# Scan stage of a four-part sequence model: which engine multiplies states 0 and 3 by C, and when the last normalization is applied

## What is computed

```python
# selective scan: D = 256 channels, N = 16 states
dt = softplus(x_ssm @ w_dt.T + b_dt)
Bm = x_ssm @ w_B.T + b_B;  Cm = x_ssm @ w_C.T + b_C
def step(h, inp):
    xt, dtt, bt, ct = inp
    h = exp(A * dtt[..., None]) * h + (dtt[..., None] * bt[:, None, :]) * xt[..., None]
    return h, sum(h * ct[:, None, :], axis=-1)          # y
pre = (y + D * x_ssm) * silu(z) @ w_out.T + b_out + x
x = layernorm(pre) * gamma + beta
# feed-forward, then the last normalization
h = layernorm(x) * ln_gamma + ln_beta
x = layernorm(x + 0.5 * (silu(h @ w1 + fc1_bias) @ w2 + fc2_bias))
```

## Time and profile before

| | |
|---|---|
| median of 3 runs | 1084.57 us (1084.56 to 1086.63) |
| the profiled execution's own time | 1086.53 us |
| its span, first to last instruction | 1084.6 us |
| busy in the span: PE, DVE, ACT, POOL | 977.9, 929.1, 839.2, 705.3 us |
| granted TensorE clock, mean | 0.968 of full speed |
| scan stage: first scan, last gate | 521.1 us, 1026.1 us |
| from one block's gates to the next's, blocks 3 to 6 | 63.4 us |

### The profile page before, as it was taken

One profiled execution on the slowest core, in us unless ns is written; L12 is line 12 of the kernel. 1 busy time (PEld: TensorE's weight loads), 2 busy tenths in 40 slices (PEclk: granted clock), 3 DMA queues, 4 the chain that ended last, 5 costly groups with the idle time before them and its releaser, 6 DMA issues. The chain is left out here.

```text
span 1084.6 us, 17899 instructions
## 1 busy us (share of the span) xinstructions
PE 977.9 (90%) x5612; PEld 741.5 (68%) x5612; DVE 929.1 (86%) x1234; ACT 839.2 (77%) x1633; POOL 705.3 (65%) x603
## 2 busy tenths in 40 slices
PE   5999999999987999998567699999999999997887
PEld 4677777777764555555456487777878777886676
DVE  7999999999973797866799998999999999999751
ACT  7777778888745668766876889899898988987733
POOL 3457466766761121123879998989999898999530
PEclk9999999999998999999887899999999999999999
DMA  6344434323425001111997867487776777767301
GB/s 190 122 139 120 127 120 142 115 92 118 123 59 196 0 1 59 59 40 67 243 157 193 162 156 188 134 195 157 162 162 159 178 160 183 173 140 161 82 1 39
DMA packets 87889, 137.53 MB, mean 127 GB/s; under 512 B 8818, under 2 KB 40562, under 8 KB 87796
## 3 DMA queue, kind: packets, MB, share of 16 engines
q1 hardware_dynamic: 86788, 132.73, 48.3%
q0 software_dynamic: 1008, 3.67, 1.7%
HBM read 120.12 MB, written 14.16 MB: 124 GB/s over the span
## 5 line engine op out<-in xcount | busy, mean ns | idle before, releaser
L2347 DVE TENSOR_TENSOR_SCAN oa<-bank_a,h,oa 128x512 f32<-128x512 f32 x128 | 159.8, 1270 | 13.2 <-ACT h L2033 9.8
L2347 DVE TENSOR_TENSOR_SCAN ob<-bank_a,h,ob 128x512 f32<-128x512 f32 x128 | 160.3, 1269 | 8.8 <-POOL ob L2567 5.3
L1829 PE MATMUL bank_m<-w,f_h 128*128 128x256 f32 x448 | 103.8, 381 | 0.0
L1491 POOL TENSOR_TENSOR oa<-ob,x1T 128x1024 f32<-128x1024 f32 x8 | 18.8, 2355 | 130.4 <-DVE ob L1391 130.4
L2024 ACT ACTIVATE bank_a<-s,A 128x512 f32<-128x512 f32 x128 | 86.8, 684 | 16.4 <-DVE oa L2347 10.2
L2024 ACT ACTIVATE bank_a<-dtc,A 128x512 f32<-128x512 f32 x128 | 86.8, 683 | 13.7 <-DVE oa L2347 8.1
L1769 PE MATMUL bank_y<-ident,ob 128*128 128x128 f32 x512 | 71.4, 285 | 25.3 <-POOL ob L2574 13.3
L1829 PEld LDWEIGHTS bank_m<-w,f_h 128*128 128x128 f32 x448 | 84.4, 192 | 14.1 <-issue 3.6
L1769 PEld LDWEIGHTS bank_y<-ident,ob 128*128 128x128 f32 x512 | 62.3, 147 | 36.6 <-DVE ob L2353 14.9
L1769 PE MATMUL bank_y<-ident,oa 128*128 128x128 f32 x512 | 72.1, 287 | 13.4 <-DVE oa L2353 13.4
L883 POOL TENSOR_TENSOR xd<-xs,L 128x512 f32<-128x512 f32 x32 | 33.9, 1061 | 76.6 <-DVE xs L662 76.1
(11 more groups left out here) (405 smaller groups left out, 2906.2 us busy)
## 6 DMA issues: line engine op xcount, KB each, us to landing
Bb<-CB_rows SPq DMA_DIRECT2D x128, 256.0 KB, 6.3
Cb<-CB_rows SPq DMA_DIRECT2D x128, 256.0 KB, 5.8
abc<-decays SPq DMA_DIRECT2D x32, 512.0 KB, 4.3
Ebc<-ramps SPq DMA_DIRECT2D x64, 128.0 KB, 3.1
uT<-in_uT SPq DMA_DIRECT2D x8, 512.0 KB, 4.2
u<-in_u SPq DMA_DIRECT2D x8, 512.0 KB, 3.9
x_tokens<-x2s SPq DMA_DIRECT2D x8, 512.0 KB, 3.0
x_rows<-x1T SPq DMA_DIRECT2D x8, 512.0 KB, 2.9
```

The source lines that it names most:

```text
L1829: i = e.matmul(to, f_h[:, k, c * CH:(c + 1) * CH], w2[:, k, :], start=False, stop=(c % 2 == 1 and k == KF - 1))
L2347: e.tensor_tensor_scan(s[:, k, :], p_a[k][:, :], s[:, k, :], h0[:, n, k:k + 1], ALU.mult, ALU.add).then_inc(v_s, 1)
```

## The change

Three edits. First, `on_pool` goes from `(0, 12, 14)` to `(3, 12, 14)`: VectorE makes product 0, GpSimd product 3. Counts of waits follow from the tuple. Second, the orders are changed to suit: on VectorE product 0 stands where product 1 stood and products 1 and 2 follow the scans of state 3, with both `stats3` ahead of them; on ScalarE the copies of C for states 0, 1 and 2 come at other places and the one for state 3 is gone; on GpSimd `into(5)` and `product(3)` come behind the scales. Third, `x3b` becomes two buffers, and `norm6` and `store_out` of blocks 0 to 4 are done in the following iteration, as four single instructions among the decays of states 12 to 14; block 5 stays where it was.

```diff
-            xl, (xn, x3b) = many("xl", [P, NC, DM]), (t(n, [P, NC, DM])[:, :, :] for n in ("xn", "x3b"))
+            xl, x3b, xn = many("xl", [P, NC, DM]), many("x3b", [P, NC, DM]), t("xn", [P, NC, DM])[:, :, :]
-            p_g, on_pool = d_sem("p_g"), (0, 12, 14)
+            p_g, on_pool = d_sem("p_g"), (3, 12, 14)
 # SyncE
                 def store_out(b):
                     e.wait_ge(a_n6, 4 * b + 4)
+                    after(e, st_o, DMAS * b)
...
                         load_B(cur, 11)
-                    if 0 <= old < NB - 2:
+                    if 0 <= it - 4 < NB - 3:
+                        store_out(it - 4)
+                    if old == Y - 1:
                         store_out(old)
 # ScalarE, first half of the iteration (older = it - 4)
+                    if 0 <= older < NB - 3:
+                        norm6(older, 0, (0,))
                     if live(post):
                         spread_C(post, 11)
                         decay(post, 12, 0)
...
                         decay(post, 12, 1)
+                    if 0 <= older < NB - 3:
+                        norm6(older, 0, (1,))
                     if 0 <= last < NB - 1:
                         evac_up(last, 0)
...
                         decay(post, 13, 0)
+                    if 0 <= older < NB - 3:
+                        norm6(older, 1, (0,))
+                    if live(post):
                         decay(post, 13, 1)
...
                         decay(post, 14, 0)
                         carry(post, 12)
+                    if 0 <= older < NB - 3:
+                        norm6(older, 1, (1,))
+                    if live(post):
                         decay(post, 14, 1)
 # ScalarE, second half
+                    if live(cur):
+                        spread_C(cur, 0)
                     if 0 <= post < NB - 1:
                         evac_gated(post, 0)
...
                         carry(cur, 1)
-                        spread_C(cur, 1)
                         decay(cur, 3, 0)
                         decay(cur, 3, 1)
                     if 0 <= last < NB - 2:
                         silu_up(last, 0)
                     if live(cur):
-                        spread_C(cur, 2)
+                        spread_C(cur, 1)
                     if 0 <= last < NB - 2:
                         silu_up(last, 1)
                     if live(cur):
                         silu_z(cur)
+                        spread_C(cur, 2)
...
                         decay(cur, 4, 1)
-                        spread_C(cur, 3)
                         carry(cur, 3)
...
                         decay(cur, 7, 0)
-                    if 0 <= old < NB - 2:
+                    if old == Y - 1:
                         norm6(old, 0)
+                        norm6(old, 1)
 # VectorE: x3b[b % 2] in second and stats6; second waits for the store of block b - 2
                     if live(cur):
-                        product(cur, 1)
+                        product(cur, 0)
...
                         residual(post, 1)
                         stats3(post, 0)
+                        stats3(post, 1)
                     if live(cur):
                         scan(cur, 3, 0)
+                        product(cur, 1)
                         scan(cur, 3, 1)
-                    if 0 <= post < NB - 1:
-                        stats3(post, 1)
-                    if live(cur):
                         product(cur, 2)
                     if live(cur):
                         scan(cur, 4, 0)
                         scan(cur, 4, 1)
-                        product(cur, 3)
                         scan(cur, 5, 0)
 # GpSimd: norm6 and norm36 of block b also wait until norm6 of block b - 1 is applied
                         into(cur, 2)
                         into(cur, 3)
-                        product(cur, 0)
                         into(cur, 4)
-                    if live(cur):
-                        into(cur, 5)
                     if 0 <= post < NB - 1:
                         shifted(post)
...
                         norm3(post)
                     if live(cur):
+                        into(cur, 5)
+                        product(cur, 3)
                         into(cur, 6)
                         into(cur, 7)
```

More of the change, by code:

```diff
@@ L1637, in store_out @@
                     e.wait_ge(a_n6, 4 * b + 4)
-                    e.dma_start(out.rearrange("(n p) f -> p n f", p=P)[:, b * NC:(b + 1) * NC, :], x3b).then_inc(st_o, DMAS)
+                    after(e, st_o, DMAS * b)
+                    e.dma_start(out.rearrange("(n p) f -> p n f", p=P)[:, b * NC:(b + 1) * NC, :], x3b[b % 2][:, :, :]).then_inc(st_o, DMAS)
                 def end_store(p):
@@ L2102, in silu_up, with norm6 @@
                     e.activation(part, part, ACT.Silu).then_inc(a_fs, 1)
-                def norm6(b, p):
+                def norm6(b, p, parts=(0, 1)):
                     if b in alone:
@@ L2108, in norm6 @@
                         e.wait_ge(p_l3, 4 * (b + 2) + 4)
-                    for c in (2 * p, 2 * p + 1):
-                        e.activation(x3b[:, c, :], x3b[:, c, :], ACT.Identity, bias=nb6[:, c:c + 1], scale=rs6[:, c:c + 1]).then_inc(a_n6, 1)
+                    for c in (2 * p + q for q in parts):
+                        e.activation(x3b[b % 2][:, c, :], x3b[b % 2][:, c, :], ACT.Identity, bias=nb6[:, c:c + 1], scale=rs6[:, c:c + 1]).then_inc(a_n6, 1)
                 def end_gated(p):
@@ L2150, in scalar @@
                 for it in range(NB + 3):
-                    old, last, post, cur, nxt = it - 3, it - 2, it - 1, it, it + 1
+                    older, old, last, post, cur, nxt = it - 4, it - 3, it - 2, it - 1, it, it + 1
                     if 0 < cur < NB:
@@ L2305, in scalar @@
                         carry(cur, 6)
-                    if 0 <= old < NB - 2:
-                        norm6(old, 1)
-                    if live(cur):
                         decay(cur, 7, 1)
@@ L2378, in second @@
                     e.wait_ge(pe_dn, 2 * b + p + 1)
-                    after(e, st_o, DMAS * b)
+                    after(e, st_o, DMAS * (b - 1))
                     for c in (2 * p, 2 * p + 1):
-                        i = e.scalar_tensor_tensor(x3b[:, c, :], xl[b % 2][:, c, :], twice4[b % 2][:, c:c + 1],
+                        i = e.scalar_tensor_tensor(x3b[b % 2][:, c, :], xl[b % 2][:, c, :], twice4[b % 2][:, c:c + 1],
                                                    pair[p][:, (c % 2) * DM:(c % 2 + 1) * DM], ALU.mult, ALU.add)
@@ L2390, in stats6 @@
                         e.wait_ge(p_l3, 4 * (b + 1) + 4)
-                    e.bn_stats(both_of(st6, p), turnwise(x3b, p)).then_inc(v_l6, 1)
+                    e.bn_stats(both_of(st6, p), turnwise(x3b[b % 2], p)).then_inc(v_l6, 1)
                 def end_low(p):
@@ L2596, in norm6 @@
                     e.wait_ge(v_l6, 2 * b + 2)
+                    after(e, a_n6, 4 * b)
                     scales(slice(NC, 2 * NC), p_l6, 4 * alone[b])
@@ L2600, in norm36 @@
                     e.wait_ge(v_l6, 2 * b6 + 2)
+                    after(e, a_n6, 4 * b6)
                     e.wait_ge(v_l3, 2 * b3 + 2)
```

## The result

The changed kernel took 1091.82 us (median of 6 runs, 1090.7 to 1093.65) against 1086.16 us (6 runs, 1084.56 to 1089.11) for the kernel before: a ratio of 1.0052, 95% interval 1.0036 to 1.0067. That is 5.7 us slower. In a second series of 10 runs it was 1.0038 (1.0023 to 1.0053), 4 us slower. The profiled execution took 1091.98 us, its span 1090.0.

The account below looks back on a forecast made before the run. GpSimd and VectorE were taken to pace the scan blocks within half a microsecond of each other. Blocks 0, 1, 2, 3 to 6 and 7 gave 0.4 + 2.4 + 0 + 1.8 + 0.8 = +5.4 us: 1090.0 us, range 1083 to 1093.

Parts of the forecast that it names:

- The sum: Whole kernel: block terms 0.4 + 2.4 + 0 + 1.8 + 0.8 make +5.4 us, 1090.0 us; chance 0.62 for +2.4 to +8.3.
- blocks 3 to 6: Steady blocks: GpSimd-VectorE loop grows +0.45 us each (bounds +0.1 and +0.75), together +1.8 us (0.4 to 3.0).
- both ranges: Kernel time 1083 to 1093 us overall, and 1087.0 to 1092.9 us for the forecast's own case.
- The loop: Steady block: scan (1, 0), VectorE's product 0, into(4), GpSimd's queue to the next into(1): 64.18 us against 63.43, +0.75.
- the small gaps: VectorE, steady block: small gaps of ScalarE's lateness; with them VectorE alone reaches `stats4` some 1.5 us sooner, otherwise at least 1.2.
- The wait at `stats4`: VectorE ahead of `stats4`: idle 1.5 to 2.5 us, released by GpSimd's `summed`.
- Block 1: Block 1: GpSimd has no wait to lose, `summed` +2.88, scan (1, 0) of block 2 +2.0 to +2.9 later; taken as +2.4.
- the lower bound: Block 1, low end: scan (1, 0) of block 2 +2.0 us later, as GpSimd's 0.82 wait ahead of into(15) may vanish.
- Block 0: Block 0: load of B hides the wait for product 0, product 3 delays into(6); +0.4 us (0 to 1).
- Blocks 2 and 7: Block 2: GpSimd's waits lost balance the added product, 0 (-0.3 to +0.3); block 7: +0.8 us (0.3 to 1.1).
- The moved normalization at nothing: Four `norm6` instructions per block among ScalarE's decays of states 12 to 14: hidden, cost nothing; uncovered up to 0.5 a block.
- The rule weighed: Closing gaps of VectorE, the busiest engine, would win 7 to 9 us (rival, chance 0.17); the loop says it does not.

Follow-up runs that it names:

- the first execution: The changed kernel (swap of products 0 and 3, normalization moved) as first profiled, against the kernel before: 1091.98 us, span 1090.0.
- the second execution: The same changed kernel profiled once more, nothing altered; span 1091.0 us.
- The earlier copy of C: Kernel before with normalization moved, plus ScalarE's copy of C for state 1 put ahead of the first evacuation of gated rows: 1084.8 us, ratio 0.9971 to the kernel before.

## Why the prediction was right

**The sum.** +5.4 us was forecast against the kernel before; +5.7 and, in the second series, +4.0 were measured. That the first came within 0.3 is in part luck: blocks 3 to 6 gave half of their term, block 7 more than its own, and single executions of one kernel differ by 4 us. 1090.0 was the forecast time, 1091.82 the measured one, inside both ranges; the difference is about that between the kernel before's median here, 1086.16, and the 1084.57 forecast from.

**The loop.** Right in its parts, for block 3: 7.58 + 0.17 for 7.60 + 0.19, the wait ahead of into(4) 3.19 (3 to 3.6 forecast; only block 2 has less, 2.70), the scales at 3.66 behind into(4) (3.62), the wait ahead of scan (4, 0) 0.52 ("under 0.5"), blocks of 63.6 to 63.7 us (63.5 to 64.2). The term was mis-sized: 55.77 for 56.36, so a block grew by 0.23 and not by 0.45. GpSimd's part gave back more than the 0.4 allowed: 0.14 ahead of the end of `summed` (24.87 for 25.01) and 0.45 behind it (30.90 for 31.35). VectorE gave back as much: from `stats4` to scan (1, 0) 30.98 for 31.60. In the kernel before it waits there for a decay behind ScalarE's second table stretch, which the prediction left among the small gaps:

```profile
744.93 1.28 DVE L2347 TENSOR_TENSOR_SCAN ob<-bank_a,h,ob 128x512 f32<-128x512 f32 x1 [0.54 <-ACT bank_a L2024]
```

With `stats4` later, that wait is covered. The 0.24 ahead of the gates stayed. Four blocks came to +0.9, not +1.8.

For blocks 3 to 6 the loop was also misnamed. The prediction closes it through into(4), yet its own sum lets the scales wait 0.30 for `stats3` behind that, so the path that it added up was already the one over `stats3`. The runs bear out the sum and not the name: the scales do follow `stats3`, and making product 0 earlier moved neither them nor, in the blocks at full clock, `stats4`.

**The wait at `stats4`.** 1.15 in block 3, below the 1.5 to 2.5 forecast. The other blocks from 1 to 6 have 1.85, 0.60, 1.27, 1.26 and 1.25. I had VectorE arrive 1.2 to 1.5 us sooner. It was there only 0.3 us sooner, since 0.51 (`add_up(3)` behind GpSimd's product 3) and 0.27 (the copy for product 4) stand in between. Neither was in the prediction. They cost nothing here, as `summed` was later still.

**Block 1.** +1.5 in the first execution, +2.5 in the second, for +2.4. `stats4` waits 1.85, `summed` starts 22.98 us behind the start of product 0, for 20.21 behind the product at that place before: +2.77, where 2.88 was worked out. Timelines of VectorE and of GpSimd in block 1:

```profile
617.32 1.30 DVE L2387 BATCH_NORM_STATS2 st<-xl 128x6 f32<-128x512 f32 x2 [1.85 <-POOL xl L2652]
...
648.24 1.28 DVE L2359 TENSOR_TENSOR_SCAN ob<-bank_a,h,ob 128x512 f32<-128x512 f32 x1 [0.30 <-POOL ob L2577]
```

```profile
593.33 2.37 POOL L2577 TENSOR_TENSOR oa<-s,Bb 128x1024 f32<-128x1024 f32 x1 [3.45 <-DVE ob L2365]
...
614.95 2.33 POOL L2652 TENSOR_TENSOR xl<-xl,s 128x1024 f32<-128x1024 f32 x1
```

The wait of 0.82 ahead of into(15) vanished, as the lower bound had it, so scan (1, 0) of block 2 came 56.27 us behind product 0 for 54.37 before: +1.9, just under the 2.0 given as the least. In the second execution it is 57.07, +2.7.

**Block 0.** +0.4 forecast, +3.0 in the first execution, +0.3 in the second. The 3.0 is the clock's late rise and not the change: the kernel with the normalization alone shows both values too (67.87 and 65.21). Blocks 0 and 1 together are +2.83 for the +2.8 of the two terms if the two executions with an early rise are compared. That close a match is luck: other pairs with like rises give +1.1 to +2.4, and the forecast stands at the upper end.

**Blocks 2 and 7.** 0 for 0. Block 7 came to +1.6 and +1.1 for +0.8 (0.3 to 1.1). VectorE's timeline there:

```profile
997.99 1.30 DVE L2387 BATCH_NORM_STATS2 st<-xl 128x6 f32<-128x512 f32 x2 [2.32 <-POOL xl L2652]
```

The wait is nearly twice that of the blocks before. I had +1.12 at `summed` less what later gaps absorb. The 0.55 between the two executions is not the swap's. It is one wait of 0.45 ahead of a product in the second half of the block, and the normalization alone has it in one execution (block of 63.12, wait 0.39) and not in the other (62.59). Like against like the swap costs 1.0 to 1.1 in this block, inside the 0.3 to 1.1 forecast. In both executions with that wait TensorE's granted clock is 0.50 just ahead of it (1007 to 1014 us in the changed kernel's); the swap alone has a stretch of half clock near that place without the wait, so what sets it off stays open.

**The moved normalization at nothing.** Right as to no cost. It even gave 0.4 us a block by itself, which the prediction didn't see. In the changed kernel this gain does not show: 63.6 with it and without it, as another loop is the longest.

**The rule weighed.** The prediction took a rule of the Trainium skill (Perfetto Trace Analysis, Optimization Strategy) to promise 7 to 9 us for the filled gap. The gap went from 1.44 to 0.52 and the block grew by 0.24, so filling it was not time won. But the page asks for something else than filling: of the wait ahead of a gap it says to "determine how to make those dependencies start sooner, or complete faster". The earlier copy of C does that. It shortens the chain on ScalarE that the gap of 1.44 waits for, and the block falls from 63.0 to 62.55; this trace agrees with the page.

## What to carry to other kernels

When a piece of work goes to another engine, follow the buffer that it frees: the engine that reuses it now waits for a place in the other's queue, with all that stands behind it. Close that loop on paper, start to start, before the gap that is filled is counted as won, and look at each wait behind it in the queue: the one that ends last is the loop, and a longer idle time further up may be slack. And where a gap's releaser has no idle time ahead of it, shorten the releaser's own chain rather than fill the gap.

## What the runs showed of the hardware

- With product 0 early, TensorE's granted clock fell to 0.50 for about 3 us behind an idle span of 2.08 us in blocks 3 and 5, in both executions, and stayed at 1.00 behind the same span in blocks 2, 4 and 6. After the 1.61 us that the changed kernel leaves at that place, and after 0.77, it stayed at 1.00 in every steady block. 1.5 us of added transposes won 1.5 us in each block that had been slow.
- Out of the long gap ahead of the stage the clock rose before 538 us in some executions and after 542 in others, of the same kernel: 64.8 or 67.5 us for block 0, and 128.0 or 129.7 for blocks 0 and 1. A stretch of half clock behind the last gates (0.50 from 1056 to 1059.4 us, in the changed kernel's second execution alone) goes with 60.67 us from there to the end for 58.97. Together such differences are as large as the 4 us over which the single times of one kernel spread.
- Where the waiting engine was idle, a hand-over from VectorE to GpSimd took 0.17 (into(4)) to 0.30 us (scales), from GpSimd to VectorE 0.03 (`stats4`) to 0.09 us (scan (1, 0) in block 1).
